# Paged attention layer on one core: output products spread over the steps, every fourth head turned by the DMA, and a new order of requests on SyncE

## The reference, cut to what matters

```python
def reference(x, subjects, table, seqlens, l0_w, Wq, Wk, Wv, Wo, q_norm_w, k_norm_w, k_cache, v_cache):
    x = x + einsum('bct,bcd->bdt', x, l0_w[subjects])          # x: 32 batches x 32 tokens x 512
    q, k, v = x @ Wq.T, x @ Wk.T, x @ Wv.T                     # 32 query heads, 8 key heads, 128 wide
    q, k = rope(rmsnorm(q, q_norm_w)), rope(rmsnorm(k, k_norm_w))
    k_all = concat(k_cache[table], k)                          # 16 pages of 32 rows = 512 old keys, 32 new keys
    v_all = concat(v_cache[table], v)
    p = softmax(where(valid, q . k_all / sqrt(128), -1e30))    # four query heads share one key head
    return x + (p . v_all) @ Wo.T                              # 32 heads x 128 wide -> 512
```

## Time and profile before

| | us |
|---|---|
| median of 3 runs | 1042.67 |
| lowest and highest run | 1039.87 and 1046.63 |
| the profiled execution, whole | 1038.51 |
| its span from first to last instruction | 1036.7 |
| its mean granted TensorE clock | 0.998 of full speed |

### The profile page before, as it was taken

One profiled execution on the slowest core, in us unless ns is written; L12 is line 12 of the kernel. 1 busy time (PEld: TensorE's weight loads), 2 busy tenths in 40 slices (PEclk: granted clock), 3 DMA queues, 4 the chain that ended last, 5 costly groups with the idle time before them and its releaser, 6 DMA issues.

```text
span 1036.7 us, 24928 instructions
## 1 busy us (share of the span) xinstructions
PE 977.4 (94%) x8329; PEld 775.4 (75%) x8329; DVE 795.4 (77%) x1706; ACT 713.1 (69%) x1943; POOL 495.6 (48%) x642
## 2 busy tenths in 40 slices
PE   3889999999889999899999999999999999999998
PEld 2678888887678788668868857866976986895793
DVE  6789999999997788757857866865875884785680
ACT  4788999988765788647846755764864774675670
POOL 6455666566881266526424623632540641552340
PEclk9999999999999999999999999999999999999999
DMA  5789999989989899768998998997999999899840
GB/s 201 252 303 337 320 384 369 384 279 399 377 289 319 313 329 356 263 186 271 344 252 260 339 266 218 330 299 203 343 295 229 308 317 240 258 359 252 239 147 11
DMA packets 268017, 296.49 MB, mean 286 GB/s; under 512 B 94065, under 2 KB 225649, under 8 KB 265329
## 3 DMA queue, kind: packets, MB, share of 16 engines
q1 hardware_dynamic: 249200, 227.65, 71.7%
q0 software_dynamic: 18688, 67.25, 18.7%
HBM read 231.77 MB, written 46.27 MB: 268 GB/s over the span
## 4 chain that ended last, share of the span: by engine, by line
PE 56%; DVE 14%; SPq 8%; DMA 6%; issue 6%; ACT 6%; POOL 3%; ACTq 0%; DVEq 0%; POOLq 0%
PE ps_o L1410 16%; PE ps_proj L1410 16%; PE ps_o L1488 8%; SPq L641 5%; PE ps_s L1448 4%; PE ps_s L1452 4%; PE ps_t L1459 3%; DMA kt<-k_pages_t 3%; DVE probs L1150 2%; PE ps_rt L1558 2%; DMA vs<-v_pages,v_row 2%; DVE c_stage L1306 1%; PE ps_o L1502 1%; DVE rot L1278 1%; DVE pt L1170 1%
## 5 line engine op out<-in xcount | busy, mean ns | idle before, releaser
L868 POOL TENSOR_SCALAR probs<-probs,recip 128x544 f32<-128x544 f32 (+1 forms) x256 | 158.4, 619 | 376.9 <-DVE recip L1158 373.0
L933 ACT ACTIVATE probs<-probs,neg_max 128x544 f32<-128x544 f32 x256 | 191.3, 747 | 158.2 <-DVE neg_max L1150 157.5
L1150 DVE CUSTOM_DVE_ANT_0 probs<-ps_s,mask,row_scale 128x544 f32<-128x544 f32 x256 | 200.1, 782 | 121.2 <-PE ps_s L1452 118.7
L1488 PE MATMUL ps_o<-pt,vs 128*128 128x128 f16 x3072 | 213.0, 219 | 5.4 <-DVE result L1192 2.5
L1488 PEld LDWEIGHTS ps_o<-pt,vs 128*128 128x128 f16 x3072 | 191.1, 98 | 16.3 <-issue 6.6
L822 POOL TENSOR_TENSOR roped<-rot 128x256 f32<-128x256 f32 x160 | 143.8, 921 | 79.4 <-DVE rot L1270 76.9
L1410 PE MATMUL ps_proj<-wt_hi,x0t_hi 128*128 128x512 f32 x384 | 158.6, 413 | 8.7 <-DVE x0t_lo L1108 7.2
L1410 PE MATMUL ps_o<-wo,ot_hi 128*128 128x512 f16 x512 | 153.5, 382 | 10.0 <-DVE ot_lo L1182 10.0
L1410 PE MATMUL ps_proj<-wt_hi,x0t_lo 128*128 128x512 f32 x384 | 150.7, 392 | 0.0
L1410 PE MATMUL ps_proj<-wt_lo,x0t_hi 128*128 128x512 f32 x384 | 149.8, 390 | 0.0
L856 POOL DMA_INDIRECT vs<-v_pages,v_row x128 | 131.7, 1029 | 22.2 <-issue 19.7
(11 more groups left out here) (145 smaller groups left out, 1590.2 us busy)
## 6 DMA issues: line engine op xcount, KB each, us to landing
kt<-k_pages_t SPq DMA_DIRECT2D x512, 128.0 KB
c_nat<-in_L_cond_k_cache SPq DMA_DIRECT2D x32, 512.0 KB, 5.8
q_t<-stage SPq DMA_DIRECT2D x64, 256.0 KB, 7.5
c_nat<-in_L_cond_v_cache SPq DMA_DIRECT2D x32, 512.0 KB, 7.0
qt<-q_t SPq DMA_DIRECT2D x32, 512.0 KB, 5.6
w_nat<-in_L_cond_Wq SPq DMA_DIRECT2D x8, 1024.0 KB, 8.4
k_pages_t<-c_stage SPq DMA_DIRECT2D x16, 512.0 KB, 5.6
c_nat<-in_L_cond_Wo SPq DMA_DIRECT2D x16, 512.0 KB, 8.1
```

What stands on the lines that cost most here:

```text
L868: pool.tensor_scalar(part, part, col(recip, i), 1.0, ALU.mult, ALU.mult).then_inc(p_norm, 1)
L933: act.activation(pr, pr, ACT.Exp, bias=col(neg_max, i), scale=-1.0, accum_out=col(row_sum, i)).then_inc(a_exp, 1)
L1150: dve.tensor_tensor_reduce(out=probs_of(i), in0=ps_s[:, score_cols(i):score_cols(i) + KEYS], in1=mask[(i // HK) % 2][:, mask_at(i):mask_at ...
L1488: ins = pe.matmul(ps_o[n % 2][:, jl * P:(jl + 1) * P], v[:, part, :], pt[i % NPT][:, NCH * half + c, :], start=jl == 0 and c == 0 and k == ...
```

## The change

The output products of a group are spread: one head (three products of 512 columns) in nearly every step from step 31 on, with two heads in two of the steps, none in the last steps of a group, and 4, 6, 6 and 16 heads in the last four steps of the last group. They add up all 32 heads in a bank of their own, `ps_y`; so only two banks (`NTB`) are left for the transposes from step 24 on. Head `i` is turned by the DMA where `i % 4 == 3` and `i >= 24` (58 heads), with a tile of its own for the split rows. `ot_hi` and `ot_lo` are laid out so that one group's quarter can be overwritten while the other group is multiplied: the 128 tokens of a head now lie 32 elements (even groups) or 8 elements (odd groups) apart. The new values' products go from 8 to 4: the low and high halves of the probabilities and a copy of the high half, made on POOL (`tn_copy`), are stacked over 96 rows. `tn_hi` and `tn_lo` become two instructions each, one step earlier. Wo's last 20 heads are converted one for every three steps, five of them on POOL. SP asks, for each batch: the transpose of head 7; queries, new keys, all 16 pages and three loads of new values of the batch after next; the transpose of the next head 3; then the rest.

```diff
-    vn = [sb(f"vn{i}", [4 * SEQ, HK // 2, 2, 2 * D], F16) for i in range(2)]
+    vn = [sb(f"vn{i}", [3 * SEQ, HK, D], F16) for i in range(2)]
...
-    ptn = [sb(f"ptn{i}", [4 * SEQ, 2, P], F16) for i in range(2)]
+    ptn = [sb(f"ptn{i}", [3 * SEQ, 2, 2, P], F16) for i in range(2)]
+    rows = sb("rows", [P, STAGED, 2, L], F16)
-    NTB = 3
+    NTB = 2
+    ps_y = psum("ps_y", [P, HID])
...
-    TN, TNE, OE = HPC - 1, HPC, HPC + 2
-    DMA_FIRST, DMA_LAST, STAGED = 2, 11, 3
+    TN, TNE, TNC, OE = HPC - 1, HPC - 1, HPC, HPC + 2
+    DMA_FIRST, T_THIRD = 24, 24
     def by_dma(i):
-        g, r = divmod(i, GSTEPS)
-        return 0 < i < NP2 and g >= 1 and (DMA_FIRST if g > 1 else 8) <= r <= DMA_LAST
+        return DMA_FIRST <= i < NP2 and i % HPC == HPC - 1
...
+    Y_AT = {r: (r + 1,) for r in range(-1, 3)} | {3: (4, 5), 4: (6, 7)} | {r: (r + 3,) for r in range(5, HQ - 3)}
+    Y_LAST = {-1: range(0, 4), 0: range(4, 10), 1: range(10, 16), 2: range(16, HQ)}
+    def head_tokens(tile, g, n):
+        if g % 2 == 0:
+            return tile[:].rearrange("p (m h) -> p m h", h=HQ)[:, :, n]
+        k, j = divmod(n, QUARTER)
+        return tile[:].rearrange("p (k m j) -> p k m j", k=GB, j=QUARTER)[:, k, :, j]
...
     def late_head(i):
-        if i >= LATE_PAIRS:
-            n = WO_EARLY + LATE_PAIRS // 2 + i - LATE_PAIRS
-        else:
-            n = WO_EARLY + i // 2 if i % 2 == 1 else HQ
-        return n if 0 <= i and n < HQ else None
+        k, r = divmod(i, 3)
+        return WO_EARLY + k if i >= 0 and r == 1 and WO_EARLY + k < HQ else None
...
     def load_new_v(b):
-                for j in range(4):
-                    width = (2 - j // 2) * D
-                    sp.dma_start(vn[s][SEQ * j:SEQ * (j + 1), :, j % 2, 0:width],
-                                 v_new[b].rearrange("t (m j) f -> j t m f", j=2)[j % 2, :, :, 0:width]
-                                 ).then_inc(d_vn[s], 16)
+                for j in range(3):
+                    part = (0, 0, 1)[j]
+                    sp.dma_start(vn[s][SEQ * j:SEQ * (j + 1)], v_new[b][:, part]).then_inc(d_vn[s], 16)
...
-            PAGES_IN = {5: 0, 6: 4, 7: 8, 0: 12}
-            for i in range(NP2):
-                if by_dma(i + 2):
-                    turn_rows(i + 2)
-                b, r = divmod(i, HK)
-                n = b + 2 if r >= 5 else b + 1
-                if 2 <= n < B and r in PAGES_IN:
-                    if r == 5:
-                        load_queries(n)
-                    load_pages(n, PAGES_IN[r], NPP // len(PAGES_IN))
-                if r == 2 and 1 <= b < B - 1:
-                    load_new_v(b + 1)
+            for b in range(B):
+                turn_rows(HK * b + HK - 1)
+                if b + 2 < B:
+                    load_queries(b + 2)
+                    load_pages(b + 2, 0, NPP)
+                    load_new_v(b + 2)
+                turn_rows(HK * (b + 1) + HPC - 1)
...
+            def tn_copy(n, normed):
+                pool.wait_ge(a_tnhi, n + 1)
+                pool.wait_ge(p_norm, normed)
+                pool.tensor_copy(ptn[n % 2][2 * SEQ:3 * SEQ], ptn[n % 2][0:SEQ]).then_inc(p_tncopy, 1)
...
-                act.activation(ptn[n % 2][0:2 * SEQ].rearrange("p m r -> p (m r)"),
-                               ps_t[tjob_no["tn", n] % NTB][0:2 * SEQ, 0:2 * P], ACT.Copy, scale=P_SCALE
-                               ).then_inc(a_tnhi, 1)
+                for e in range(2):
+                    ins = act.activation(ptn[n % 2][0:SEQ, e], turned_new(n, e), ACT.Copy, scale=P_SCALE)
+                ins.then_inc(a_tnhi, 1)
...
-                for m in range(2):
-                    for e in range(2):
-                        v = vn[b % 2][:, 2 * h + m, e]
-                        jl = 2 * m + e
-                        for part in range(2):
-                            ins = pe.matmul(ps_o[n % 2][:, jl * P:(jl + 1) * P], v[:, part * D:(part + 1) * D],
-                                            ptn[n % 2][:, m, :], start=False, stop=m == 1 and e == 1 and part == 1,
-                                            skip_group_check=True)
+                for jl in range(HPC):
+                    m, e = divmod(jl, 2)
+                    ins = pe.matmul(ps_o[n % 2][:, jl * P:(jl + 1) * P], vn[b % 2][:, HPC * h + jl, :],
+                                    ptn[n % 2][:, e, m, :], start=False, stop=jl == HPC - 1, skip_group_check=True)
...
+            def project_out(g, n):
+                h = head_at(g, n)
+                hi, lo = head_tokens(ot_hi, g, n), head_tokens(ot_lo, g, n)
+                ins = products(ps_y[:], [(hi, wo[:, h, 0, :]), (hi, wo[:, h, 1, :]), (lo, wo[:, h, 0, :])],
+                               first=n == 0, last=n == HQ - 1)
...
+                for n in y_heads(i):
+                    project_out(y_group(i), n)
```

193 lines of the change are left out of this document (102 added, 91 removed).

## The result

The changed kernel takes 1087.2 us (median of 4 runs, 1078.91 to 1098.58), the kernel before 1041.85 us beside it (4 runs). The ratio is 1.0402, with a 95% interval of 1.0328 to 1.0476: slower by 4%, where 1017 us was forecast and 1048 was the top of the range. The profiled execution took 1085.94 us, its span is 1084.2 us, 73 more than the 1011 of the forecast.

A forecast was written before the change was run, and what follows sets the result against it. PE was taken to bound the kernel: 997 us, plus 11 for late SP and 3 for short steps at group ends, gave a 1011 us span; 1013 with 1.8 outside, 4.2 more for the median: 1017 us, range 1001 to 1048.

The forecast's parts named there:

- the sum of SP's chain: SP's requests from head 7's rows to head 3's landing: 17.8 to 18.7 us a batch, against 18.0 before PE's use.
- it lands 4.2 us after its issue: Landing of head 3's DMA transpose, last part of SP's requests: 4.2 us, range 2.9 to 8.3.
- first rival: Transposes land 5.8 us after issue among value gathers; SP late 1.4 to 2.3 us a batch, 1045 to 1070 us; chance 0.17.
- The issue terms: SP's issues between heads 7 and 3: transpose 1.25 us, queries, new keys and pages 10.8 or 11.7, new values about 1.5.
- the 11 allowed: Loss for SP's late transposes: 0.4 us a batch over 28 batches, 11 us.
- the term's bound of +3 on the old pace: Steps 0 to 31 keep their pace of 2.157 us a step, changing by -1 us, bounds -4 and +3.
- the 3 us of corners: Two output-free steps at each group's end are shorter than DVE's work there: 0.4 us a group, 3 us in all.
- PE's own sum: PE's work: 9.83 us per four steps, 19.65 a batch, 78.6 a group, its end of the span at 997 us.
- The strided weight loads: Loads of `ot_hi` and `ot_lo` for output products: hidden up to 0.216 us, taken at no cost; bounds nothing and 34 us.
- The second rival: Strided weight loads slower than 216 ns: at 392 ns 135 us more, 1150 in all; milder about 1050; chance 0.14.
- the one of the seams paid for DVE: PE waits for DVE where new keys are turned and split: up to 35 us, about 1040 us; chance 0.06.
- Two banks at nothing: Two transpose banks instead of three, emptied by ACT and DVE in time: no cost, bounds 0 and 0.2 us a step.

The follow-up runs named there:

- tiny pages: Changed kernel with each key page's DMA moving 8 of 128 partitions from the third batch on, value gathers kept: 1062.44 us (one run).
- half rows in even steps: Changed kernel with value gathers split into half rows, one in each of a batch's eight steps: 1073.3 us, ratio 1.0313.

## Why the prediction was wrong

**The step that failed** is the sum of SP's chain, and in it the term "it lands 4.2 us after its issue". Measured to the value products, it is 6.65 us in the mean for head 3 (5.0 to 10.1 where PE waited for it), and 8.0 to 11.4 for the eight heads 7 that came late, which the forecast didn't count at all. The 4.2 was the median over the kernel before, in which the DMA heads stand together in 10 of 32 steps. Head 3's transposes now meet the value gathers in nearly every batch (POOL issues four of them at 636.39 to 642.81 around the transpose of 637.70), which the forecast itself said in its first rival, with 5.8 us. The late heads 7 come just behind the gathers: in all eight the batch's last one was issued 0.4 us before. The run without gathers settles it: 2.8 us of landing, no loss.

**A second error in the same step** is where the chain starts, but it cost nothing. The forecast counted from DVE's rows of head 7. With one tile for both heads the start in a late batch is the value products of head 3, which are what the landing delays, and all of the circle becomes the length of the batch. By size the two readings differ little: the forecast's own sum with the measured terms is 14.5 + 6.65 = 21.2 us against 18.0, late by 3.2 a batch or 89 us, where the circle gives 2.9 and 82; and the kernel with a tile of its own for head 7 is no faster. So the forecast would have come out near 1095 us with the landing right. The issue terms were right (13.6 to 14.5 forecast for transpose, requests and new values, 14.5 measured).

**The sum put right**: 28 x (22.57 - 19.65) = 81.8 us in place of the 11 allowed, and 4.4 more before step 31 (425.2 for 420.8), just past the term's bound of +3 on the old pace; one wait of 2.3 us for DVE, at the change to two banks in step 24, is in it. 1011 + 70.8 + 4.4 = 1086, less the 3 us of corners, which the circle hides, makes 1083; the span is 1084.2.

**What was right.** PE's own sum: pieces, output products 0.22 apart, the tail (1057.1 to the start of the last product at 1080.1 is 23.0, to its end 23.1 was forecast), and 997 us against 1005.8 without the gathers. The seams are gone. The strided weight loads take 147 ns for 98 and stay below 216:

```profile
L1444 PEld LDWEIGHTS ps_y<-wo,ot_hi 128*128 128x128 f16 x512 | 57.0, 147 | 7.0 <-issue 0.8
```

The Trainium skill (Advanced Engine Details and Errata, Memory Cachelines) names a penalty for such accesses. The trace agrees: a load takes some 49 ns more, at 64 as at 16 bytes between the columns, and it is hidden. No run changed the layout alone. The second rival fell. So did the one of the seams paid for DVE, and `tn_copy` cost nothing.

**Which rival held.** The first, SP late, at a larger size: it said 1045 to 1070 us for 1.4 to 2.3 us a batch, and it is 2.9 us. Two banks at nothing was right only beside the DMA heads; without them they cost 109 us, far above the bound of 0.2 us a step (45 us), which no sentence of the forecast made depend on them.

**What was in the rows and not read.** The earlier trace rows has DMA busy 0.99 at 284 GB/s in a steady group. The kernel before moves 280 GB/s in 602 to 872, in batches of 20.9 us; the changed one 242 in 22.57, that is 5.5 MB a batch. In 19.65 us this would be 278 GB/s: the DMA would have had to be as fast as in the kernel before, in a kernel whose transposes come at worse moments. No step of the forecast asked that. Busy share alone isn't a bound, though: tiny pages had 0.70 and were late.

**What stays open.** That the gathers make the landings late is shown; why they hurt more than pages of the same bytes is argued from packet sizes, and the one direct test, half rows in even steps, gained about 1%, not clear of noise. Whether an order exists that has both rows and pages in time with the gathers in flight: none of those tried has.

## What to carry to other kernels

Where one tile or one queue serves a transfer and then its own next issue, add up the whole circle (issue, everything queued between, landing, use) and compare it with the period; a median landing from another place in the kernel is no term for it, only one read beside the traffic that the new place has. A small-packet transfer on the critical path wants a moment in which the large ones don't move, and a queue of its own can make it worse. When one late item is found in a loop, look whether its neighbours are late too: here a third of the waits were for the other head. When a change takes a buffer (here a PSUM bank) from one stage, ask which other edit of the same change pays for it, because the two can't be judged apart.

## What the runs showed of the hardware that was not expected

- A DMA transpose of 0.26 MB (5.25 MB for 20 issues) lands in 2.8 us (median) when no gathers are in flight, in 13.3 us (median) on a queue of its own beside pages and gathers, and in 9.4 us (median) behind queries and four pages in SP's queue. The Trainium skill (Advanced Engine Details and Errata, X-Bar Transpose (TRN2)) calls transposes as fast as regular DMAs; alone they may be, under traffic these were not: 1056 packets of 0.25 KB took 16.3% of the engines for 5.25 MB, SP's other transfers 44.8% for 30.55 MB, twice the share for a megabyte.
- The issue of a transpose on SP, 1.25 us as a rule, takes 4.39 us in the row above, where twelve pages were asked for just ahead of it.
- Two transpose banks instead of three: PE waits for DVE 4.8 us with 8 jobs in each eight steps, 53.3 with 9 and 109 with 10. The waits come with each four steps that hold five jobs, about 2 us for each, and hardly at all where there are four.
